# Second normalisation of 24 token tiles in each expert layer: from VectorE to ScalarE, in two steps

## The reference

```python
def _layernorm(x, axis=-1, eps=1e-05):
    m = jnp.mean(x, axis=axis, keepdims=True)
    v = jnp.var(x, axis=axis, keepdims=True)
    return (x - m) / jnp.sqrt(v + eps)
...
    scores = sigmoid(x @ w_gate.T)                # 16 experts in 4 groups
    # 2 of 4 groups by the sum of their two best, then 4 experts of them, weights normalised
    routed = jnp.einsum('tef,ehf,te->th', silu(x @ w1_e) * (x @ w3_e), w2_e, combine)
    shared = _swiglu(x, w1_s, w3_s, w2_s)
...
    x = x + 0.5 * _L0_ffn_ref(_layernorm(x), ...)         # first expert layer
    x = x + _L0_attn_ref(_layernorm(x), ...)
    x = x + 0.5 * _L0_ffn_ref(_layernorm(x), ...)         # second expert layer
    x = x + 0.5 * _L1_ffn_ref(_layernorm(x), ...)
    x = x + _L1_attn_ref(_layernorm(x), ...)
    x = x + 0.5 * _L1_ffn_ref(_layernorm(x), ...)
```

## Time and profile before

| | |
|---|---|
| median of three runs | 2573.61 us (2571.7 to 2576.8) |
| the profiled execution | 2570.51 us |
| its span, first to last instruction | 2568.5 us |
| PE busy | 2141.2 us, 83% |
| DVE busy | 1551.2 us, 60% |
| ACT busy | 970.2 us, 38% |
| POOL busy | 317.8 us, 12% |
| mean granted TensorE clock | 0.900 |

### The profile page before, as it was taken

How to read it: one execution, slowest core, us unless ns; L and a number is a source line. 1 busy time by engine, 2 the same in 40 slices (tenths; PEclk the granted TensorE clock), 3 DMA queues, 4 the chain that set the end, 5 groups by cost and what they waited for, 6 DMA issues and landing times.

```text
span 2568.5 us, 38687 instructions
## 1 busy us (share of the span) xinstructions
PE 2141.2 (83%) x12842; PEld 1602.7 (62%) x12842; DVE 1551.2 (60%) x4452; ACT 970.2 (38%) x1961; POOL 317.8 (12%) x298
## 2 busy tenths in 40 slices
PE   5589999957999955899999456578998998999856
PEld 3478888846788834788888335434445544554445
DVE  7744434446455577443443698576876776778286
ACT  4122332322333342233232233235555555555532
POOL 4320000031000044100000432311002002000000
PEclk8699999978999977999999656579999999999956
DMA  8110111020000031101110210422322422422001
GB/s 258 39 67 24 30 30 30 26 64 25 1 1 1 1 115 55 53 26 30 30 30 26 83 51 25 74 44 58 51 27 57 69 27 57 70 27 27 2 25 49
DMA packets 84037, 114.84 MB, mean 45 GB/s; under 512 B 12213, under 2 KB 73817, under 8 KB 80729
## 3 DMA queue, kind: packets, MB, share of 16 engines
q1 hardware_dynamic: 77416, 94.80, 16.8%
q0 software_dynamic: 6432, 17.57, 2.1%
HBM read 69.16 MB, written 43.17 MB: 44 GB/s over the span
## 4 chain that ended last, share of the span: by engine, by line
PE 61%; DVE 27%; ACT 5%; issue 4%; DMA 2%; POOL 1%; DVEq 0%; ACTq 0%; SPq 0%; POOLq 0%
PE psum L783 10%; PE psum L785 10%; PE psum L784 10%; PE psum L126 5%; PE psum L2306 4%; PE psum L127 4%; PE psum L128 4%; DVE mt L2194 3%; PE psum L2285 3%; PE psum L870 3%; DVE m L2182 2%; DVE stats L160 2%; PE psum L2265 2%; DVE m L2191 2%; DVE xn L185 2%
## 5 line engine op out<-in xcount | busy, mean ns | idle before, releaser
L2145 ACT ACTIVATE pt<-psum 128x512 f32<-128x512 f32 (+3 forms) x768 | 333.9, 493 | 274.7 <-DVE psum L2220 180.3
L748 DVE SCALAR_TENSOR_TENSOR h<-psum,xg,sg 128x128 f32<-128x128 f32 x592 | 166.9, 344 | 415.4 <-PE psum L870 415.3
L557 ACT ACTIVATE sg<-psum 128x512 f32<-128x512 f32 x180 | 107.5, 597 | 573.5 <-PE psum L785 573.5
L783 PE MATMUL psum<-w_hi,xt_hi 128*128 (+1 forms) x720 | 285.7, 397 | 32.8 <-DVE xt_lo L713 32.8
L784 PE MATMUL psum<-w_lo,xt_hi 128*128 (+1 forms) x720 | 284.1, 395 | 0.0
L785 PE MATMUL psum<-w_hi,xt_lo 128*128 (+1 forms) x720 | 283.8, 394 | 0.0
L2265 PE MATMUL psum<-ks,qs 96*128 96x512 bf16 (+3 forms) x768 | 235.3, 346 | 36.7 <-DVE m L2182 10.3
L2285 PE MATMUL psum<-qs,ks 99*128 99x512 bf16 (+3 forms) x768 | 238.6, 334 | 24.7 <-ACT pt L2145 19.0
L783 PE MATMUL psum<-w_hi,ht_hi 128*128 (+1 forms) x720 | 219.3, 305 | 0.2
L2194 DVE CUSTOM_DVE_ANT_0 mt<-psum,band_q 128x256 bf16<-128x256 f32 (+1 forms) x512 | 204.1, 399 | 18.5 <-PE psum L2265 8.3
L2289 PE MATMUL psum<-band,ident_r 128*128 128x256 f32 (+1 forms) x864 | 214.9, 337 | 0.0
(11 more groups left out here) (286 smaller groups left out, 4485.7 us busy)
## 6 DMA issues: line engine op xcount, KB each, us to landing
xg<-w_dram SPq DMA_DIRECT2D x54, 256.0 KB, 3.3
qk_scr<-parts SPq DMA_DIRECT2D x32, 384.0 KB, 2.5
qs<-qk_scr SPq DMA_DIRECT2D x96, 128.0 KB, 7.1
ks<-qk_scr SPq DMA_DIRECT2D x96, 128.0 KB, 7.8
xg<-rows_in SPq DMA_DIRECT2D x74, 132.0 KB, 2.2
rows_out<-yb SPq DMA_DIRECT2D x74, 128.0 KB, 1.7
x<-x_dram SPq DMA_DIRECT2D x4, 1024.0 KB, 8.7
out_dram<-x SPq DMA_DIRECT2D x4, 1024.0 KB, 4.5
```

The lines of the kernel that those rows point to most:

```text
L748: ins = dve.scalar_tensor_tensor(out=h[i % 2][:, e, :], in0=u[:, e, :], scalar=xg[j % XSLOT][:, at:at + 1], in1=sg[i % 2][:, e, :], op0=AL ...
L783: pe.matmul(out, a[0], b[0], start=first, stop=False)
L2145: act.activation(pt[n % NPT][:, 0:q1 - q0], st_bank(n)[:, 0:q1 - q0], ACT.Exp).then_inc(*exped.up())
```

## The change

DVE's part of "again" is only the copy of `w8`, signalled by `weighed`; the four normalisations of L185 are gone for chunks 0 to 5 (24 tiles in each expert layer). ACT gets a part in "again": four activations that add the negative mean, a wait for its own signal `shifted`, four that multiply by `rstd` in place, and the signal `renormed`. The first one waits for `routed`, which DVE's last operation of `route_weights` gives. PE's transposes and POOL's scatters wait for `renormed` where they waited for `normed`, and POOL for `weighed` besides. The list `moe_order` is as it was.

```diff
+            routed, shifted, renormed = S("routed"), S("shifted"), S("renormed")
...
-                            pool.wait_ge(*(normed(NCH + i + 1) if i < NCH - 2 else weighed(i - (NCH - 2) + 1)))
-                            if i >= NCH - 2:
+                            pool.wait_ge(*weighed(i + 1))
+                            if i < NCH - 2:
+                                pool.wait_ge(*renormed(i + 1))
+                            else:
                                 pool.wait_ge(*S.dma(f"fetched{i % 2}")(1))
...
+                        elif kind == "again" and i < NCH - 2:
+                            if i == 0:
+                                act.wait_ge(*routed(1))
+                            if i >= 4:
+                                act.wait_ge(*S.dma(f"scattered{i % 4}")(CT))
+                                act.wait_ge(*turned(KD * (NCH + i - 3)))
+                            for t in range(CT):
+                                at = slice(i * CT + t, i * CT + t + 1)
+                                ins = act.activation(xn[i % 4][:, t, 0:D], X[:, i * CT + t, :], ACT.Identity,
+                                                     bias=minus_mean[:, at])
+                            ins.then_inc(*shifted.up())
+                            act.wait_ge(*shifted(i + 1))
+                            for t in range(CT):
+                                at = slice(i * CT + t, i * CT + t + 1)
+                                ins = act.activation(xn[i % 4][:, t, 0:D], xn[i % 4][:, t, 0:D], ACT.Copy,
+                                                     scale=rstd[:, at])
+                            ins.then_inc(*renormed.up())
...
-                        then(dve.tensor_reduce(w8[:, :, n * EG:(n + 1) * EG], mix.rearrange("p t g k -> p t k g"),
-                                               AXIS.X, ALU.add))
+                        ins = dve.tensor_reduce(w8[:, :, n * EG:(n + 1) * EG], mix.rearrange("p t g k -> p t k g"),
+                                                AXIS.X, ALU.add)
+                        if n == 0:
+                            then(ins)
+                    ins.then_inc(*routed.up())
+                    dve.wait_ge(*routed(1))
...
                         elif kind == "again":
                             if i >= 4:
                                 dve.wait_ge(*S.dma(f"scattered{i % 4}")(CT))
-                                dve.wait_ge(*turned(KD * (NCH + i - 3)))
-                            ins = dve.tensor_copy(xn[i % 4][:, :, D:ROW], w8[:, i * CT:(i + 1) * CT, :])
-                            if i < NCH - 2:
-                                norm(i, xn[i % 4][:, :, 0:D])
-                            else:
-                                ins.then_inc(*weighed.up())
+                            dve.tensor_copy(xn[i % 4][:, :, D:ROW],
+                                            w8[:, i * CT:(i + 1) * CT, :]).then_inc(*weighed.up())
...
-                            pe.wait_ge(*normed(n + 1))
+                            pe.wait_ge(*(normed(n + 1) if n < NCH else renormed(n - NCH + 1)))
```

## The result

| | before | changed |
|---|---|---|
| median, 22 runs each | 2573.47 us (2566.59 to 2577.68) | 2579.4 us (2572.89 to 2583.78) |
| ratio | | 1.0025, 95% interval 1.0017 to 1.0032 |
| profiled execution / its span | 2570.51 / 2568.5 us | 2580.66 / 2578.9 us |
| mean granted TensorE clock | 0.900 | 0.903 |
| DVE busy / ACT busy | 1551.2 / 970.2 us | 1533.5 / 1009.7 us |

The change makes the kernel slower, by 0.25%, that is 6.4 us (4.4 to 8.2 by the interval). The forecast was 2582.3 us in a range of 2577.5 to 2587.0, with 0.86 for slower.

What follows compares the result with a forecast made beforehand. DVE was taken to set the time before unit 4. Per layer 13.3 - 4.2 + 0.7 - 5.2 - 0.3 = 4.3 us, second layer 4.4; 2573.61 + 8.7 = 2582.3 us, range 2577.5 to 2587.0.

Steps and rivals of the forecast that it cites:

- What is removed: DVE's queue before unit 4: 16 normalisations of chunks 0 to 3 go, taking 5.2 us off in each layer.
- what is added: ACT's queue before the silu of unit 3: 32 activations from 104.90 us, 3.33 us a chunk, 13.3 us for four.
- What is queued behind it: After ACT's block: silu and `h` of unit 3, then `xt_lo` and PE's unit 4, late by 4.3 us.
- The rule for the change: Skill's rule on saturated DVE: by it alone each layer would win 5.2 us, -10.4 us in sum; weighed and not followed.
- Later chunks: Chunks 4 and 5: ACT's eight activations stay hidden before PE releases the silu of unit 5, 0.27 us to spare; cost nothing.
- POOL and the fetches: Scatters and sorted-row fetches: chunks 4 and 5 late by 4.3 us and a few tenths, 16 us of room, not on the path.
- The clock: PE's restart before unit 4: already at 0.50, longer idling costs no lower level; nothing taken, 0.6 us a layer kept for range.
- The sum: Both expert layers: 4.3 + 4.4 = 8.7 us lost, giving 2582.3 us; this case, ACT in the way, had chance 0.84.
- the term from `h` to `xt_lo`: DVE's queue behind `h` of unit 3: `ht_lo`, additions to X, "table" and `xt_lo` again take 4.29 us without a wait.
- tighter activations: Rival 2, ACT's block: activations 0.27 us apart, four chunks 9.3 us, each layer loses 0.3 us; 2574.2 us, chance 0.07.
- a free DVE: Rival 3, before unit 4: ACT's work doesn't hold DVE, 5.2 us come out in each layer; 2563.2 us, chance 0.03.
- activations without overlap: Rival 4, ACT's block: 4.0 us a chunk, 16.0 for four, later chunks +0.4 twice a layer; 2589.3 us, chance 0.06.

## Why the prediction was right, step by step

**What is removed** held: 5.2 us left DVE's queue, and the four copies stand behind each other. So did **what is added**, almost to the digit: a chunk was to take 3.33 us and took 3.32 to 3.35, four 13.3 and took 13.34; the gap of ACT's wait for itself, taken as 0.04, was 109.70 - (107.97 + 1.71) = 0.02 us, and 0.03 in the next three chunks. Page-wide the two forms run at 497 and 496 ns, as in the earlier trace rows.

**What is queued behind it.** `h` was forecast 14.07 us after `t0` and came at 14.06; DVE was to idle some 9 us for the silu and idled 9.46. From `h` to `xt_lo` the forecast repeated before's 4.29 us; it took 4.06, since the small operations of "table" (L671 to L682 before, L695 to L706 after) took 2.19 us in place of 2.43. That term was mis-sized: 4.05 and 4.08 us a layer in place of 4.3 and 4.4, 8.1 in all in place of 8.7. PE's wait was to be about 12 us and was 12.78 and 12.87; 4.1 of the 4.9 us are the later `xt_lo`, the rest is that PE was done with its transposes earlier: it began to wait at 127.47 - 12.78 = 114.69, that is `t0` + 6.8, where before it was 120.32 - 7.84 = 112.48, `t0` + 7.7.

**The rule for the change.** DVE was busy 9.51 of 10 us in the routing, and the 5.2 us did leave its queue; but DVE then idled 9.46 us for ACT, and each layer lost 4.1 us. The Trainium skill, "Perfetto Trace Analysis", section "Optimizing Scalar/DVE Operations", says that with DVE saturated moving some work to ScalarE may make sense; taken alone, that gave a gain of 5.2 us a layer, which this trace doesn't show. With half of the work moved, DVE and ACT ran side by side and unit 4 came 2.5 us earlier; with the order changed, 5.3 us earlier. So moving work paid here as long as what stood on ACT ahead of the operations that others wait for was no longer than what DVE had left to do.

**Later chunks** held: in both layers the silu of unit 5 was still released by PE, with 0.19 us of idle time where 0.27 were forecast, and that of unit 7 with 0.20. **POOL and the fetches** held in what counts: nothing at the sorted tiles waited for them, and the delay there, 4.47 / 3.55 us, is about that of unit 4. The scatters of chunk 4 came 3.3 and 2.6 us later after `t0`, not 4.3 and a few tenths: before, they had stood behind the sixteen of the burst. **The clock** held: PE restarted at 0.50 of full speed, and from its start to the silu of unit 4 it took 0.24 us more in the first layer and 0.56 less in the second, within the 0.6 kept for it.

**The sum** was 8.7 us, the traces show 8.0 to 8.1, the timed runs 6.4 (4.4 to 8.2). So the mechanism was right and the amount a third too large, above the interval; 0.5 us of that is the term from `h` to `xt_lo`, and where the other 1.7 us between the traces and the timed runs went isn't shown. Of the rivals, tighter activations (0.40 us apart, not under 0.32), a free DVE and activations without overlap all fell at the first timeline. The prediction's number rests on before's median of 2573.6, which the 22 runs gave as 2573.47; on chips where before takes 2590 us the same change reads 1.0014, and no step of the prediction provided for that.

## What to carry to other kernels

Moving work to an idle engine is paid for by what stands behind it in that engine's queue, not by how idle the engine is: sum the moved block up to the first operation that another engine is waiting for, and compare it with the lead that this operation had (here 16 us of lead, of which 9.8 could be used after `t0`, against 13.3 us of block). The same 48 activations a layer made the kernel 0.25% slower in one block and, spread between ACT's other steps and with a pause in the scatters, 0.54% faster than before on a chip without the standstill. Before a gain in one stretch is booked, look at the next rendezvous on the same chip, since a standstill there can take it all.

## What the hardware showed that I had not expected

- The same kernel takes about 2573 us in two sets of runs (2573.47, 2572.23) and about 2590 on three other chips (2590.71, 2589.79, 2591.22), at nearly the same granted clock (0.899 to 0.905 in all traces). Each of the four chips on record ran one set, and the chip of the first result isn't on record, so whether this belongs to the chip or to the hour isn't shown.
- On the slower chips ACT and DVE stand still for up to 13 us in each expert layer while POOL issues 12 or 16 indirect scatters back to back. PE's work for them is done, but PE's semaphore updates are recorded up to 13.0 us late; ACT goes on 2.2 to 2.9 us after the last scatter (once 1.2), also where that burst is put off. The end of the last idle time follows the burst in all nine traces, and some late signals come amid it; what causes the delay isn't shown.
- The same late signals of PE stand in the attention layer between the two expert layers, where POOL gathers the sorted rows back: in the slow trace of before up to 9.6 us late at 599.1 to 599.4, after a long run of gathers (L1029) that ends at 596.7. This goes with the rest of the difference: from ACT's first operation there to its first of the second expert layer it is 362.1 us in that trace and 354.1 in the first one, beside about 6 us in each expert layer up to the sorted tiles. In that stretch DVE's own updates are late too, by up to 1.9 us over the nine traces.
